# The first norm of the second layer run inside the first layer's last batch, and waits written in another order

## What is computed

```python
# layer 0, attention: latent kv, 16 heads of 8, one rotary part (32) shared by all heads, causal
xn = _layernorm(x); c_kv = xn @ W_kv_down
scores = q k^T + q_rope k_rope^T; w = softmax(mask(scores / sqrt(8 + 32)))
x_attn = (w v) @ W_o
# layer 0, soft mixture: 8 experts with 64 slots each
xf = rmsnorm(xn) ; logits = xf @ rmsnorm(slot_embeds)^T          # 512 tokens x 512 slots
dispatch = softmax(logits, over tokens); combine = softmax(logits, over slots)
eo = gelu(dispatch^T xf @ w1 + b1) @ w2 + b2
x1 = x + x_attn + combine @ eo
# layer 1, attention: latent kv, 16 heads of 64, causal; 16 experts, top 8 of a sigmoid gate, one shared
xn = _layernorm(x1)
out = x1 + attention(xn) @ w_out + sum_e gate_e * silu(xn w_gate_e) * (xn w_up_e) @ w_down_e + shared expert
```

## Time and profile before

| | before |
|---|---|
| median of 3 runs | 2973.04 us (2971.9 to 2975.1) |
| the profiled execution: time, span | 2973.48 us, 2971.8 us |
| first layer, second layer (from the span's start) | to about 1145.9 us, from there |
| one batch of the first layer, of the second | 68.13 us, 111.05 us |
| TensorE busy in one batch | 63.32 us, 109.50 us |

### The profile page before, as it was taken

One profiled execution on the slowest core, in us unless ns is written; L12 is line 12 of the kernel. 1 busy time (PEld: TensorE's weight loads), 2 busy tenths in 40 slices (PEclk: granted clock), 3 DMA queues, 4 the chain that ended last, 5 costly groups with the idle time before them and its releaser, 6 DMA issues.

```text
span 2971.8 us, 71998 instructions
## 1 busy us (share of the span) xinstructions
PE 2792.8 (94%) x27076; PEld 1596.6 (54%) x27076; DVE 2399.3 (81%) x4452; ACT 2074.8 (70%) x4411; POOL 1542.5 (52%) x1355
## 2 busy tenths in 40 slices
PE   5999999999999996999999999999999999999998
PEld 2555555555555553555555555555555555555554
DVE  6777777777777776888888888888888888888886
ACT  3777777677677765777777777777777777777764
POOL 2333333333333333665666666666666666666664
PEclk8999999999999998999999999999999999999999
DMA  4222222222222224454454464464454454454452
GB/s 126 59 55 55 66 67 56 68 58 57 55 58 61 55 55 128 109 142 113 115 145 118 110 148 115 111 150 113 111 149 113 112 149 112 112 146 115 111 147 69
DMA packets 272089, 298.15 MB, mean 100 GB/s; under 512 B 30848, under 2 KB 235648, under 8 KB 271488
## 3 DMA queue, kind: packets, MB, share of 16 engines
q1 hardware_dynamic: 247424, 274.70, 37.0%
q10 hardware_dynamic: 24320, 18.85, 2.0%
HBM read 141.39 MB, written 25.69 MB: 56 GB/s over the span
## 4 chain that ended last, share of the span: by engine, by line
PE 48%; DVE 6%; issue 3%; ACT 2%; DMA 1%; POOL 1%; SPq 0%; ACTq 0%; DVEq 0%; POOLq 0%
PE l_ps_out L1703 7%; PE l_ps_any L1592 5%; PE l_ps_any L1593 5%; PE l_ps_any L1594 5%; PE l_ps_exp L1684 4%; PE l_ps_any L1740 4%; PE l_ps_exp L1686 4%; PE l_ps_any L1749 4%; PE l_ps_any L1659 3%; PE l_ps_sum L1725 2%; PE l_ps_exp L1688 2%; PE l_ps_any L1664 1%; PE l_ps_any L1586 1%; DVE l_yT L1533 1%; DVE l_select L1431 1%
## 5 line engine op out<-in xcount | busy, mean ns | idle before, releaser
L1268 POOL TENSOR_TENSOR stage<-l_p_in,stage 128x512 f16<-128x512 f32 x640 | 759.3, 1198 | 405.5 <-ACT l_p_in L1381 404.5
L695 DVE TENSOR_REDUCE neg_max<-ps_any 128x1 f32<-128x384 f32 (+3 forms) x704 | 413.2, 635 | 118.3 <-PE ps_any L824 117.9
L1377 ACT ACTIVATE stage<-l_ps_exp 128x512 f16<-128x512 f32 x640 | 388.2, 607 | 157.3 <-PE l_ps_exp L1688 135.9
L1277 POOL TENSOR_TENSOR l_hid<-l_hid,l_spread 128x512 f32<-128x512 f32 x256 | 340.8, 1336 | 247.4 <-DVE l_hid L1546 211.8
L555 ACT ACTIVATE probs<-ps_exp 128x512 f32<-128x512 f32 x640 | 348.0, 605 | 95.4 <-PE ps_exp L839 90.6
L469 POOL TENSOR_SCALAR_AFFINE_SELECT probs<-probs 128x512 f32<-128x512 f32 x256 | 165.4, 664 | 441.6 <-ACT probs L555 441.6
L1381 ACT ACTIVATE l_p_in<-l_ps_exp 128x512 f32<-128x512 f32 x640 | 390.3, 610 | 0.0
L1513 DVE TENSOR_REDUCE l_neg_max<-l_ps_any 128x2 f32<-128x768 f32 (+2 forms) x384 | 310.9, 863 | 17.0 <-PE l_ps_any L1664 13.9
L822 PE MATMUL ps_any<-k_st,q_st 120*128 120x128 f16 (+3 forms) x1024 | 255.6, 305 | 70.8 <-DMA k_st<-stack_scratch 43.8
L1684 PE MATMUL l_ps_exp<-l_q_a,l_k_a 128*128 128x512 f16 (+3 forms) x1024 | 304.8, 300 | 3.2 <-DMA l_q_b<-l_max_row 1.6
L1686 PE MATMUL l_ps_exp<-l_q_b,l_k_b 66*128 66x512 f16 (+3 forms) x1024 | 295.5, 300 | 0.0
(11 more groups left out here) (262 smaller groups left out, 6739.1 us busy)
## 6 DMA issues: line engine op xcount, KB each, us to landing
l_spread<-route_scratch SPq DMA_DIRECT2D x128, 512.0 KB, 5.0
l_q_a<-l_q_hi SPq DMA_DIRECT2D x256, 128.0 KB, 2.4
l_y_rec<-rec_scratch SPq DMA_DIRECT2D x128, 256.0 KB, 4.6
l_q_b<-l_q_lo SPq DMA_DIRECT2D x128, 128.0 KB, 2.4
l_k_a<-l_k_hi SPq DMA_DIRECT2D x128, 128.0 KB, 2.6
l_k_a<-l_k_lo SPq DMA_DIRECT2D x128, 128.0 KB, 2.8
l_k_b<-l_k_hi SPq DMA_DIRECT2D x128, 128.0 KB, 2.7
q_st<-rot_hi SPq DMA_DIRECT2D x64, 128.0 KB
```

Of the source, the lines that this page charges most:

```text
L695: nc.vector.tensor_reduce(neg_max[:, n % 2, heads[0]:heads[0] + k, t], src, AX.X, ALU.max, negate=True).then_inc(drained["dve"], 1)
L1268: nc.gpsimd.tensor_tensor(probs[:, n % 2, 1, u], p_in[:, m % P_SLOTS], probs[:, n % 2, 0, u], ALU.subtract).then_inc(p_lo_ok.sem, 1)
L1277: nc.gpsimd.tensor_tensor(at, at, spread[:, c % 3, n % SPREAD], ALU.mult).then_inc(weighted.sem, 1)
L1377: nc.scalar.activation(probs[:, n % 2, 0, u], bank, ACT.Exp, scale=float(HD1) ** -0.5).then_inc(exp_done.sem, 1)
```

## The change

1. `layer0_program` puts a step `first_norm` before the last batch's `combine` 0 and a step `first_scale` behind its `combine` 3. They hold the norm and the scaling of the second layer's batch 0; in layer 1 these steps run for the other batches only. The small tiles and semaphores move to `Early`.
2. The five late loads are issued by SP at the start of layer 1 instead of ScalarE.
3. The mask casts go from VectorE to GpSimd, ahead of its two memsets.
4. `high_weights` and `low_weights`: three weights, then xn_p's halves, then the rest. TensorE waits for 3 (and 4) halved weights instead of for 4 at once.
5. In both layers waits are dropped where another implies them, and put in another order.

```diff
+    last = steps.index(("combine", batches - 1, 0))
+    after = steps.index(("combine", batches - 1, 3)) + 1
+    return (steps[:last] + [("first_norm", batches - 1, 0)] + steps[last:after] + [("first_scale", batches - 1, 0)]
+            + steps[after:])
...
+                if name == "first_scale":
+                    act.wait_ge(early.stats_ok.sem, early.stats_ok.at(0, 2 * TB + 2))
+                    for t in range(TB):
+                        nc.scalar.activation(early.x_in[:, t], early.x_in[:, t], ACT.Identity, bias=early.shift[:, t:t + 1],
+                                             scale=early.rstd[:, t:t + 1]).then_inc(early.xn_ok.sem, 1)
...
-                    nc.scalar.activation(w[:, n], full(act, f"logits{name[4:]}{b}_{n}"), ACT.Exp, bias=neg[:, n:n + 1],
+                    logits = ps_any[:, banks.at[f"logits{name[4:]}{b}_{n}"]]
+                    nc.scalar.activation(w[:, n], logits, ACT.Exp, bias=neg[:, n:n + 1],
...
                 if name == "exp":
                     u, g = which[1], G * b + n
+                    act.wait_ge(exp_full.sem, exp_full.at(g, u + 1))
                     if u == 0 and g >= 2:
                         act.wait_ge(pv_done.sem, pv_done.at(g - 1, 0))
-                    act.wait_ge(exp_full.sem, exp_full.at(g, u + 1))
...
                 if name == "hidden":
                     if b == 0 and n == 0:
                         act.wait_ge(late_loaded, all_late)
+                    bank = full(act, f"hidden{b}_{n}")
                     if b and n == 0:
                         filling(act, f"expert_out{b - 1}")
-                    bank = full(act, f"hidden{b}_{n}")
...
+                if name == "first_norm":
+                    dve.wait_ge(early.x_loaded.sem, early.x_loaded.at(0, 16))
+                    for t in range(TB):
+                        nc.vector.bn_stats(early.stats[:, t], early.x_in[:, t]).then_inc(early.stats_ok.sem, 1)
...
+                if name == "first_scale":
+                    dve.wait_ge(early.rstd_ok.sem, early.rstd_ok.at(0, 1))
+                    nc.vector.scalar_tensor_tensor(out=early.shift[:], in0=early.mv[:, :, 0], scalar=-1.0,
...
-                    emptied(pe, f"xfT{b}")
+                    if n == 0:
+                        emptied(pe, f"xfT{b}")
...
         def _(sp):
+            for parts, sem in zip(late_loads, (up_loaded, down_loaded, out_loaded)):
+                for dst, src in parts:
+                    sp.dma_start(dst, src).then_inc(sem, 16)
...
+            pool.wait_ge(early.loaded, early.all)
+            nc.gpsimd.tensor_copy(ident_h[:], ident[:]).then_inc(cast_ok, 1)
+            nc.gpsimd.tensor_copy(later_h[:], masks[:, 0:2]).then_inc(cast_ok, 1)
+            nc.gpsimd.tensor_copy(mask_h[:], masks[:, 2]).then_inc(cast_ok, 1)
...
-            high_weights(split_in[:4])
+            high_weights(split_in[:3])
...
-                bank = full(dve, name)
                 dve.wait_ge(sem.sem, count)
+                bank = ps_any[:, banks.at[name]]
...
                 if name == "xnT":
                     low_part(f"xnT{b}", xn_p[:, b % 2, 1], xn_p[:, b % 2, 0], X_SCALE, x_hi_ok, x_hi_ok.at(b, 1))
+                if name == "xnT" and b == 0:
+                    low_weights(split_in[3:], 3)
...
                 if name in ("lat", "gate", "qk") and b == 0:
-                    pe.wait_ge(weights_lo, len(split_in) - 1)
+                    pe.wait_ge(weights_lo, 3)
+                if b == 0 and (name == "v" or name == "qk" and step[3] >= 2):
+                    pe.wait_ge(weights_lo, 4)
...
+                    pe.wait_ge(p_lo_ok.sem, p_lo_ok.at(p, 5))
                     if p:
                         pe.wait_ge(y_ok.sem, y_ok.at(p, 0))
```

More of the change, by code:

```diff
@@ L661, in _ @@
                 if name == "slots":
-                    bank = full(dve, f"slots{b}")
+                    bank = ps_any[:, banks.at[f"slots{b}"]]
                     dve.wait_ge(slots_hi.sem, slots_hi.at(b, 1))
@@ L709, in _ @@
                 if name == "combine":
-                    bank = full(dve, f"combine{b}_{n}")
+                    bank = ps_any[:, banks.at[f"combine{b}_{n}"]]
                     dve.wait_ge(turned_hi.sem, turned_hi.at(b, 4 + n + 1))
@@ L1400, in _ @@
                 nc.vector.memset(ones_in[:, j, j:j + 1], 1.0).then_inc(prep, 1)
-            def casts():
-                nc.vector.tensor_copy(ident_h[:], ident[:]).then_inc(prep, 1)
-                nc.vector.tensor_copy(later_h[:], masks[:, 0:2]).then_inc(prep, 1)
-                nc.vector.tensor_copy(mask_h[:], masks[:, 2]).then_inc(prep, 1)
-                for r in range(2):
-                    rows = slice(HD1 * r, HD1 * r + HD1)
-                    nc.vector.tensor_copy(ident_2[rows], ident[rows, rows]).then_inc(prep, 1)
             def low_weights(parts, first):
@@ L1464, in _ @@
                     low_weights(split_late[1:], len(split_in) + 1)
-                if name == "norm":
+                if name == "norm" and b:
                     dve.wait_ge(x_loaded.sem, x_loaded.at(b, 16))
```

82 lines of the change are left out of this document (46 added, 36 removed).

## The result

| | before | after |
|---|---|---|
| median | 2972.94 us (2971.9 to 2975.1) | 2933.47 us (2931.07 to 2933.76) |
| ratio, 95% interval | | 0.9867 (0.9855 to 0.9879) |
| the profiled execution: time, span | 2973.48, 2971.8 us | 2933.48, 2931.8 us |
| first layer ends at | 1145.9 us | 1114.6 us |
| second layer takes | 1825.9 us | 1817.2 us |

The change saves 39.5 us. The two spans differ by 40.0 us: 31.3 in the first layer, where 18.5 were forecast (20.6 - 2.1), and 8.7 in the second, where 7.0 were (5.4 + 1.6).

The account below looks back on a forecast made before the run. TensorE was taken as the bound, busy 63.32 of 68.13 us per first-layer batch and 109.50 of 111.05 in the second. Terms -20.6 + 2.1 - 5.4 - 1.6 = -25.5 gave 2947.5 us, range 2938 to 2963.

Parts of the forecast that it names:

- Part 1: First layer, ScalarE's table loads in each batch: reordered or dropped waits let both start earlier, saving 20.6 us.
- exp half: First layer, soft_c: dropping the logits wait ahead of the exp table load saves 0.53 us a pass.
- gelu half: First layer, hidden: asking for the hidden bank before the old expert_out saves 0.80 us a pass.
- Part 4: Fewer or reordered waits elsewhere: 0.05 us at two TensorE waits in each second-layer batch, saving 1.6 us.
- where an engine is busy they cost nothing: Separate waits on VectorE, TensorE and ScalarE: free on a busy engine, costing only where the engine waits.
- Part 2: First layer's last batch: ScalarE's scaling for the second layer's norm stands ahead of y_un and costs 2.1 us.
- that clock: Granted clock falling in the longer pause before the first layer's last products: 2 to 3 us more, outside the sum.
- Part 3: Second layer's start: reordered casts and halves bring VectorE's route 8.4 us after the layer's start, saving 5.4 us.
- rival C: Second layer: shifted phase makes VectorE and POOL slow each other, 33 us lost, 2980 us; chance 0.05.
- A: First layer: table load cannot start nearer than 0.90 us behind an activation; 6.1 instead of 20.6, 2962 us; chance 0.15.
- B: First layer: table load needs its own pause of 1.3 us or more; table-load gain nothing, 2968 us; chance 0.10.

Follow-up runs that it names:

- the two shifts: The kernel before with all first-layer tiles 224 bytes further (2957.94 us, ratio 0.9948), and with them 96 bytes further (ratio 0.9946).

## Why the prediction was wrong

**Part 1, the table loads: the mechanism right, the size a little small.** 20.6 us forecast, 20.9 measured alone. The separate wait ahead of the load was the cause, and no pause stands behind it. The exp half came out to 0.02 us; the gelu half was 0.2 a pass too small, since the idle time ahead of a product is not all that its wait costs. The period fell by 1.56 and not by 1.34, so the total agrees more closely than the term did.

**The step that failed: the place of the tiles, taken as nothing.** My part list had no term for it; the small tiles' move stands among the changes only as a fact. It is worth 0.9 us a pass, 13.5 to 16 us, about the whole miss of 14.0. The profile of before could not show it as a loss: the wait for k_st looked like any DMA wait, and I followed it only to ask what starts the loads, not how long they last. What would have led there is the address of each tile that a DMA on the critical path reads, before and after.

**Part 4 and "where an engine is busy they cost nothing": wrong both ways.** The 1.6 us for reordered waits in the second layer don't show (0.6 the other way, inside the spread). In the first layer the dropped waits bring 0.1 us a pass and take 5 to 6 us back, by way of TensorE's instruction fetch, which I hadn't thought of as something that a count of waits can move.

**Part 2, the scaling ahead of y_un: the delay right, the price mis-sized.** 2.1 forecast, 2.3 measured, and 2.9 for the clock on top. The forecast had named that clock and its 2 to 3 us (without a row for them) among the things that would make it wrong, but left it out of the sum, though it had put the whole tail behind y_un itself.

**Part 3, the start of the second layer: right.** The route starts at 8.25 (8.4 forecast), 5.5 us earlier from the layer's start than before. The second layer as a whole is 8.4 shorter on average of the twelve kernels with the old start and the seven with the new (1824.9 against 1816.5): 5.5 for the start and 3.4 for the batches from the third on, less 0.5 elsewhere. Most of the 3.4 are up to three late ones: all twelve kernels with the old start have at least one batch of 112 us there, none of the seven with the new one has, whatever their waits. In the profile of before VectorE is busier in them, in one kind of operation (1.3 to 1.5 us more on l_hw), the kind of thing that rival C feared, but one that was there before and went. Why it went stays open, and the forecast had no term for it: its 7.0 for the second layer came near the measured 8.7 by a term that doesn't exist (1.6) in the place of one that it lacked.

The sum as it should have stood: -20.9 for the loads, -14.8 for the place (mean of the two shifts, by medians), +5.2 for the scaling, -8.4 for the second layer, and for the other waits of the first layer what they measured alone, +2.5: -36.4 to the measured -39.5. The loads' and the place's terms are known to some 5 us each, so the sum can't tell more closely. Of the rivals, A and B fell with the idle time ahead of the loads, C with the second layer's period. My range took in only terms that I had. Its lower end, 2938, was even lower than the bounds that it names give (20.6 - 1.3 + 8 + 3.2 = 30.5, so 2942.5), and the place of the tiles was outside all of them.

## What to carry to other kernels

Treat a moved allocation as an edit of its own: list the start of every tile that a DMA on the critical path reads, and keep it on a multiple of 128 bytes, or measure that it doesn't matter there. When a pass stands in a loop, look at its late passes as well as at one in the middle; a wait that grows from some pass on, at full clock, points at something that slides, and the instruction fetch is one such thing, so a list made shorter is not safely faster. Put work that nobody waits for behind the last short chain of a layer, not ahead of it: the idle time it makes also costs the clock.

## What the runs showed of the hardware

- The loads that read rows of 1 KB from SBUF tiles starting 32 or 64 bytes behind a multiple of 128 moved 614 to 625 packets in 3 us, and 654 to 658 when the tiles started on a multiple of 128 (128 or 0 behind one of 256). The start of the tiles written to made next to no difference (614, with the sources 32 behind).
- One packet of TensorE's instruction fetch (16 KB) held one DMA engine for some 1.3 us inside a full load; one issue of SyncE took 1.93 us instead of 0.56, and TensorE's wait 2.08 us instead of 0.64.
- An ACT_TABLE_LOAD of 1.28 us starts 0.02 us behind the last activation, if no separate wait ahead of it is still open.
- A wait ahead of a TensorE product cost 0.40 us where it showed 0.24 of idle time: the product also lost its overlap with the one ahead of it.
- TensorE at 2.4 GHz went to 1.2 GHz after 2.97 us idle behind its last values and stayed there for eleven of the twelve products of the last result (0.43 instead of 0.21 us each); after 0.72 us idle it did not. Pauses of 0.77 to 0.96 us a little earlier were followed by it in five kernels and not in four.
